# Sixteen-head attention: 1/sum applied to the head outputs on GpSimd instead of to the probabilities

## The chip, the cores and the metric

The kernel runs on one core of a Trainium2 chip. The metric is the device time of one execution, in microseconds (us); three runs of the kernel before gave 1747.81 us (median; 1742.91 to 1748.35). The change is judged by the median of the kernel after against that.

## What is computed

Four conditioned blocks follow one another on x of 16 batches x 256 rows x 256 columns, in float32. The change touches only the second one's attention, with 16 heads of 64:

```
h = _modulate(_layernorm(x), sh_msa, sc_msa)
q, k, v = jnp.split(h @ W_qkv, 3, axis=-1)               # to (batch, 256, 16 heads, 64)
attn = jax.nn.softmax(einsum('bqhd,bkhd->bhqk', q, k) * 64 ** -0.5, axis=-1)
out = einsum('bhqk,bkhd->bqhd', attn, v).reshape(batch, 256, 1024)
x = x + g_msa * (out @ W_out + b_out)
```

The softmax divides each row of exp(score - max) by the row's sum. A row belongs to one query q and one head, so the division may as well be made on that query's and head's output.

## The kernel before, in words

Five engines run instruction lists of their own and meet at semaphores: TensorE (PE), VectorE (DVE), ScalarE (ACT), GpSimd (POOL) and SyncE (SP, which issues all DMAs). Each list is in order: an instruction that waits holds up everything behind it on its engine. float32 matmuls are made of three passes over a high and a low part (`hi`, `lo`), so most results are read out of PSUM twice, by ACT (the `hi` copy) and by DVE (`lo` = value - `hi`).

The attention is written as a software pipeline of 128 periods, n = 8 b + j, for batch b and head pair j = 0 to 7. In period n each engine does, in this order:

- PE (`mh_tensor`): the first half of the transposes of pair n's probabilities (`pair_transpose`, L1086), the scores of pair n+2 (`pair_scores`, L1019), the other half of the transposes, the projections due in this period (q and k of one pair in each; in j = 1, 2, 5, 6 also a quarter of V), in j = 3 the transposes of the next batch's rows, the output projection of pair n-3, and the values of pair n-1 (`head_values`).
- ACT (`mh_scalar`, L1279): `o_read` of pair n-2 (L1148, two copies of 64 partitions out of PSUM into `oc`), `pt_read` of pair n (L1115, two), the four exponentials of pair n+2 (L1055; each also yields a row sum in `rsum`; in j = 3 `rows_scalar`, L1221, stands in the middle of them), then `proj_scalar`, the `hi` copies of the period's projections (L995 for q and k, L1003 for V).
- DVE (`mh_vector`, L1304): 1/sum of pair n+1 (`prob_inverse`, L1064), in j = 3 `res_vector` (L1186), the row maxima of pair n+2 (`score_max`, L1045), `o_add` of pair n-2 (two additions, L1157, then the rounded copy `oThi`, L1161), `pt_rest` of pair n (L1120, two), in j = 3 `rows_vector` (L1232, L1235), `proj_vector` (L1012, L1017), in j = 1 `ln_stats` (L353, L359), in j = 2 `ln_norm` (L376), in j = 4 `weights_hi` (L327).
- POOL (`mh_gpsimd`, L1339): four multiplications of the probabilities of pair n+1 by `rinv` (`prob_weigh`, L1083), and `o_rest` of pair n-2 (L1166), beside small work in j = 2 to 5. In the last two periods ACT does two of the four multiplications (`prob_weigh_act`, L1076).
- SP (`mh_sync`, L1363): only in j = 0, two weight slices (L313) and one gate row (L1209).

Waits that matter: the first transposes of a period wait for the weighed probabilities and for `pt_rest` of the pair before (`pt_lo`); the scores of pair n+2 wait for the exponentials of pair n+1 (their two PSUM banks are single); `score_max` waits for the scores; the exponentials wait for `score_max`; `o_add` waits for both copies of `o_read` (`o_corr`) and, one pair back, for `o_rest` (`o_lo`); `head_values` waits for the `o_add` of the pair before in the shared bank (`o_sum`).

Of the kernel before, what the change touches and what calls it, by code (L numbers as in the profile page):

```python
# [15 lines left out]
ALU = mybir.AluOpType  # L16
# [27 lines left out]
def bass_cond_blocks(nc, t, out):  # L44
# [57 lines left out]
    GROUP_BASE = before(lambda q: GROUPS if q in HID else 0)  # L102

    gate_scratch = nc.dram_tensor("gate_scratch", (NPH, BATCH, 2 * D), F32).ap()

    ctx = ExitStack()
    with ctx:
# [59 lines left out]
        rsum = [sb(f"rsum{i}", [P, 2 * TPB], scope=att) for i in range(2)]  # L167
        rinv = [sb(f"rinv{i}", [P, 2 * TPB], scope=att) for i in range(2)]


        front_a, front_b = DC * HID[0] + HID[0] // P * D, DC * HID[1] + HID[1] // P * D
# [51 lines left out]
        ln_xn = sem("ln_xn"); ln_tp = sem("ln_tp"); ln_nf = sem("ln_nf"); ln_lo = sem("ln_lo"); ln_full = sem("ln_full"); prob_act = sem("prob_act"); pt_half = sem("pt_half")  # L223
# [4 lines left out]
        x_new = sem("x_new"); x_tmp = sem("x_tmp"); x_stored = sem("x_stored")  # L228

        o_corr = sem("o_corr"); o_sum = sem("o_sum"); q_scaled = sem("q_scaled")  # L230
        proj_mm = sem("proj_mm"); proj_hi = sem("proj_hi"); proj_lo = sem("proj_lo")
        v_hi = sem("v_hi"); v_lo = sem("v_lo"); s_mm = sem("s_mm"); max_ready = sem("max_ready")
# [802 lines left out]

        def of_head(tiles, h):

            return tiles[h // 2 % 2][:, h % 2 * TPB:(h % 2 + 1) * TPB]

        def score_max(dve, n):  # L1040

# [6 lines left out]
        def score_exp(act, h):  # L1048

            act.wait_ge(nmax_ready, h - h % 2 + 2)  # L1050
            if h >= 4:
                act.wait_ge(pt_mm, h - 3)
                act.wait_ge(rinv_ready, h - h % 2 - 2)
# [12 lines left out]
        SHARED = 2  # L1066

        def weighed(h):

            return h - max(h // 2 - (PERIODS - SHARED), 0)  # L1070

        def prob_weigh_act(act, h):

            act.wait_ge(rinv_ready, h - h % 2 + 2)
            for q in range(TPB):
                last = act.activation(prob[h % 4][:, q, :], prob[h % 4][:, q, :], ACT.Copy, scale=of_head(rinv, h)[:, q:q + 1])  # L1076
            last.then_inc(prob_act, 1)

        def prob_weigh(pool, h):

            pool.wait_ge(rinv_ready, h - h % 2 + 2)
            for q in range(TPB):
                last = pool.tensor_scalar(prob[h % 4][:, q, :], prob[h % 4][:, q, :], of_head(rinv, h)[:, q:q + 1], None, ALU.mult)  # L1083
            last.then_inc(prob_ready, 1)

        def pair_transpose(pe, n, turn):  # L1086

            if n == 0:
                pe.wait_ge(y_taken, GB * GROUP_BASE[A])
            if turn == 0:  # L1090
                pe.wait_ge(prob_ready, weighed(2 * n + 2))
                if n >= PERIODS - SHARED:
                    pe.wait_ge(prob_act, n - (PERIODS - SHARED) + 1)
                if n:
                    pe.wait_ge(pt_lo, 2 * n)
            else:
                pe.wait_ge(pt_half, 2 * n + 2)
            for c in range(TPB):
                for q in range(TPB):
                    both = []  # L1100
                    for h in range(2):
                        r = (h + turn) % 2
                        rows = slice(r * HALF, (r + 1) * HALF)
                        at = c * SEQ + q * P + r * HALF
                        both.append(pe.transpose(PTB[h][:, at:at + HALF],  # L1105
                                                 prob[(2 * n + h) % 4][rows, q, c * P:(c + 1) * P], ident[rows, rows]))
            for ins in both:
                ins.then_inc(pt_mm if turn else pt_half, 1)
# [38 lines left out]
                main, rest, cols = o_halves(j)  # L1147
                act.activation(oc[main, :], OB[rest, cols], ACT.Copy).then_inc(o_corr, 1)  # L1148

        def o_add(dve, pair, i):  # L1150

            if pair:
                dve.wait_ge(o_lo, pair)
            for j in range(2):
                main, _, cols = o_halves(j)
                dve.wait_ge(o_corr, 2 * pair + 2)
                dve.tensor_tensor(of[main, :], OB[main, cols], oc[main, :], ALU.add).then_inc(o_sum, 1)  # L1157
            dve.wait_ge(o_sum, 2 * pair + 2)
            if pair >= 2:
                dve.wait_ge(out_mm, pair - 1)  # L1160
            dve.tensor_copy(oT[i][0][:, :], of[:, :]).then_inc(o_hi, 1)  # L1161

        def o_rest(pool, pair, i):

            pool.wait_ge(o_hi, pair + 1)
            pool.tensor_tensor(oT[i][1][:, :], of[:, :], oT[i][0][:, :].bitcast(F32),  # L1166
                               ALU.subtract).then_inc(o_lo, 1)

        def out_project(pe, pair, j, b):
# [109 lines left out]
        def mh_scalar(act, b, j):  # L1279

            n = PAIRS * b + j
            if n >= 2:
                o_read(act, n - 2)
            if PERIODS > n + 1 >= PERIODS - SHARED:
                prob_weigh_act(act, 2 * n + 3)
            for h in range(2):
                pt_read(act, 2 * n + h)
            if n + 2 < PERIODS:
                score_exp(act, 2 * n + 4)
            if j == NEXT - 1 and b + 1 < BATCH:  # L1290
                act.wait_ge(proj_mm, item(b, ("qk", PAIRS - 1)) + 1)
                rows_scalar(act, b + 1)
            if n + 2 < PERIODS:
                score_exp(act, 2 * n + 5)
            for it in items(b, j):
                proj_scalar(act, *it)
            if b == BATCH - 1 and j in (PAIRS - 3, PAIRS - 2):
                act.wait_ge(proj_mm, NPROJ * BATCH)
                head_unit("scalar", act, A + 1, j - (PAIRS - 3))
            if n == PERIODS - 1:  # L1300
                o_read(act, n - 1)
                o_read(act, n)

        def mh_vector(dve, b, j):  # L1304

            n = PAIRS * b + j
            if n + 1 < PERIODS:
                prob_inverse(dve, n + 1)
            if j == 3 and b:
                res_vector(dve, A, b - 1, YB, out_mm, PAIRS * b, b - 1)  # L1310
            if n + 2 < PERIODS:
                score_max(dve, n + 2)
            if n >= 2:
                o_add(dve, n - 2, n % 2)
            for h in range(2):
                pt_rest(dve, 2 * n + h)
            if j == NEXT - 1 and b + 1 < BATCH:
# [14 lines left out]
                for k in range(GB):  # L1332
                    head_unit("vector", dve, A + 1, k)
            if n == PERIODS - 1:
                o_add(dve, n - 1, (n - 1) % 2)
                o_add(dve, n, n % 2)
                res_vector(dve, A, b, YB, out_mm, PAIRS * b + PAIRS, b)

        def mh_gpsimd(pool, b, j):  # L1339

            n = PAIRS * b + j
            if n + 1 < PERIODS:
                prob_weigh(pool, 2 * n + 2)
            if j == 2 and b + 1 < BATCH:
                ln_rsqrt(pool, A, b + 1, 0)
            if b == BATCH - 1 and j == NEXT - 1:
                head_norms("gpsimd", pool, A + 1)
            if n + 1 < PERIODS - SHARED:
# [7 lines left out]
            if j == NEXT + 1:  # L1356
                res_gpsimd(pool, b, b)
            if n == PERIODS - 1:
                o_rest(pool, n - 1, (n - 1) % 2)
                o_rest(pool, n, n % 2)  # L1360
                res_add(pool, b, b)

        def mh_sync(sp, b, j):  # L1363

            if j:
                return
            weights_load(sp, A + 1, b)
            gate_load(sp, A, b, b)


        def mh_start(name, eng):
            if name == "gpsimd":
                for h in range(2):
                    prob_weigh(eng, h)
                return
            f = {"tensor": proj_tensor, "scalar": proj_scalar, "vector": proj_vector}[name]

# [13 lines left out]
            f(eng, 0, ("qk", 2))  # L1391
            if name == "tensor":
                pair_scores(eng, 1)
            if name == "vector":
                prob_inverse(eng, 0)
            head_pair(1)
            f(eng, 0, ("v", 0, 1))
            f(eng, 0, ("qk", 3))
# [28 lines left out]
        def sh_transpose(pe, b):  # L1427

            n = H0 + b
            pe.wait_ge(prob_ready, weighed(H0) + b + 1)  # L1430
# [32 lines left out]
        def sh_scale(dve, b):  # L1463

            dve.wait_ge(exp_ready, H0 + b + 1)
            dve.wait_ge(prob_ready, weighed(H0) + b - 1)
            if b >= 2:
                dve.wait_ge(prob_ready1, b - 1)
            dve.reciprocal(rinv[0][:, 0:TPB], rsum[0][:, 0:TPB]).then_inc(rinv_ready, 1)
            dve.wait_ge(rinv_ready, H0 + b + 1)  # L1470
# [332 lines left out]
```

## Time and profile before

| | us |
|---|---|
| median of three runs | 1747.81 |
| span of the profiled execution | 1752.5 |
| sixteen-head attention in it, about | 256 to 1012 |
| PE busy in the span | 1626.4 (93%) |
| DVE / ACT / POOL busy | 1294.3 / 1179.8 / 1093.6 |

The profile is of one execution. Besides totals it offers a chain of work that ended last (each step followed back to what released it), groups of instructions by line, a timeline by engine, and busy times of chosen stretches. The view of the DMAs gives issues and the time from issue to landing.

### The profile page before, as it was taken

What the parts mean: (1) busy time and instruction counts of PE and PEld (TensorE: products, weight loads), DVE (VectorE), ACT (ScalarE), POOL (GpSimd) and SP (SyncE); (2) the same over time, 40 slices, a digit from 0 to 9 for tenths busy, and PEclk for the clock granted to TensorE, in tenths of its full rate; (3) what the DMA queues carried; (4) which work ended last, traced back from release to release, by engine and by line L of the source; (5) the groups of instructions that cost most, each with busy time, mean ns of one, the idle gap of its engine ahead of it and who ended that gap; (6) DMA issues with size and microseconds to landing.
All of it is one profiled execution on the core that took longest, in us unless ns stands there. A gap on an engine that the chain in (4) does not pass through costs nothing.

```text
span 1752.5 us, 37390 instructions
## 1 busy us (share of the span) xinstructions
PE 1626.4 (93%) x13251; PEld 1458.4 (83%) x13251; DVE 1294.3 (74%) x2766; ACT 1179.8 (67%) x2896; POOL 1093.6 (62%) x1261
## 2 busy tenths in 40 slices
PE   4888998999999999999999789999999999989997
PEld 2557878888888888888888779999888889989997
DVE  3767768989898888888888745556788778864442
ACT  2545657777787777787777655556676667666663
POOL 1555667888888888888888622333555568842223
PEclk7999999999999999999999899999999999999999
DMA  8213310000000000000000011111122112221111
GB/s 306 61 49 86 88 42 11 11 10 11 11 7 6 11 10 11 11 11 11 10 11 10 1 32 30 31 31 32 48 57 58 45 27 46 47 52 37 37 49 48
DMA packets 110973, 65.93 MB, mean 38 GB/s; under 512 B 81530, under 2 KB 92788, under 8 KB 110788
## 3 DMA queue, kind: packets, MB, share of 16 engines
q1 hardware_dynamic: 110788, 63.54, 13.3%
q8 instruction: 107, 1.75, 0.4%
q14 instruction: 78, 0.64, 0.1%
HBM read 59.06 MB, written 4.46 MB: 36 GB/s over the span
## 4 chain that ended last, share of the span: by engine, by line
PE 64%; DVE 13%; issue 8%; POOL 6%; ACT 2%; DMA 0%; DVEq 0%; POOLq 0%; SPq 0%; ACTq 0%
PE bank L289 14%; PE bank L290 13%; PE bank L291 13%; POOL prob L1083 5%; PE s_banks L289 4%; PE bank L1105 4%; DVE ptlo L1120 4%; PE s_banks L290 4%; PE s_banks L291 4%; PE s_banks L1028 4%; PE bank L1131 3%; DVE of L1157 2%; PE bank L417 2%; DVE xn L376 2%; DVE oThi L1161 1%
## 5 line engine op out<-in xcount | busy, mean ns | idle before, releaser
L1083 POOL TENSOR_SCALAR prob<-prob,rinv 128x256 f32<-128x256 f32 x508 | 465.8, 935 | 117.0 <-DVE rinv L1064 117.0
L1055 ACT ACTIVATE prob<-s_banks,nmax 128x256 f32<-128x256 f32 x512 | 236.6, 475 | 17.4 <-DVE nmax L1045 17.4
L289 PE MATMUL bank<-WBhi,hl 128*128 128x256 f32 x768 | 219.0, 285 | 6.2 <-DVE upd L647 5.3
L290 PE MATMUL bank<-WBlo,hh 128*128 128x256 f32 x768 | 217.7, 283 | 0.0
L291 PE MATMUL bank<-WBhi,hh 128*128 128x256 f32 x768 | 215.5, 281 | 0.0
L1115 ACT ACTIVATE pthi<-bank 128x512 fp32r<-128x512 f32 x256 | 139.2, 596 | 100.9 <-PE bank L1105 98.8
L1045 DVE TENSOR_REDUCE nmax<-s_banks 128x4 f32<-128x1024 f32 x128 | 156.0, 1219 | 62.6 <-issue 61.9
L610 ACT ACTIVATE hh<-bank,vecs 128x512 fp32r<-128x512 f32 x120 | 82.9, 691 | 155.7 <-PE bank L291 155.7
L430 ACT ACTIVATE nThi<-bank,mod 128x256 fp32r<-128x256 f32 x192 | 110.5, 575 | 104.9 <-issue 75.7
L289 PE MATMUL bank<-aThi,WAlo 128*128 128x256 f32 x576 | 175.4, 304 | 0.6 <-DVE aTlo L438 0.2
L1120 DVE TENSOR_TENSOR ptlo<-bank,pthi 128x512 fp32r<-128x512 f32 x256 | 164.9, 686 | 4.0
L616 DVE TENSOR_TENSOR hl<-bank,hh 128x512 fp32r<-128x512 f32 x120 | 82.5, 688 | 112.3 <-ACT bank L610 111.2
L290 PE MATMUL bank<-aTlo,WAhi 128*128 128x256 f32 x576 | 161.6, 281 | 0.0
L289 PEld LDWEIGHTS bank<-WBhi,hl 128*128 128x128 f32 x768 | 145.8, 190 | 18.7 <-issue 9.7
L291 PE MATMUL bank<-aThi,WAhi 128*128 128x256 f32 x576 | 161.1, 280 | 0.0
L1105 PE MATMUL bank<-ident,prob 64*128 64x64 f32 x2048 | 113.9, 228 | 45.2 <-DVE ptlo L1120 23.4
L290 PEld LDWEIGHTS bank<-WBlo,hh 128*128 128x128 f32 x768 | 145.8, 190 | 7.2
L1105 PEld LDWEIGHTS bank<-ident,prob 64*128 64x128 f32 x2048 | 92.6, 139 | 67.1 <-POOL prob L1083 37.1
L376 DVE TENSOR_SCALAR xn<-x,meanvar,rstd 128x256 f32<-128x256 f32 x224 | 123.6, 610 | 31.4 <-POOL rstd L368 31.4
L291 PEld LDWEIGHTS bank<-WBhi,hh 128*128 128x128 f32 x768 | 146.5, 191 | 0.0
L1131 PE MATMUL bank<-ptlo,vv 128*128 128x256 f32 x512 | 129.8, 286 | 7.2 <-DVE of L1157 7.2
L616 DVE TENSOR_TENSOR hl<-s_banks,hh 128x512 fp32r<-128x512 f32 x120 | 81.6, 680 | 72.6 <-ACT s_banks L610 72.6
(185 smaller groups left out, 5546.5 us busy)
## 6 DMA issues: line engine op xcount, KB each, us to landing
gates<-gate_scratch SPq DMA_DIRECT2D x96, 256.0 KB, 3.6
agate<-gate_scratch SPq DMA_DIRECT2D x32, 256.0 KB, 3.6
stage<-in_L_cond_W SPq DMA_DIRECT2D x64, 64.0 KB, 2.3
out<-x SPq DMA_DIRECT2D x16, 256.0 KB, 2.2
adaw<-in_L_cond_Wc SPq DMA_DIRECT2D x1, 3072.0 KB, 17.7
stage<-in_L_cond_W_qkv SPq DMA_DIRECT2D x8, 384.0 KB, 3.4
x<-in_x SPq DMA_DIRECT2D x1, 2560.0 KB, 16.6
stage<-in_L_cond_ff_w SPq DMA_DIRECT2D x32, 64.0 KB, 2.2
```

The costliest lines, as they stand in the source:

```text
L289: pe.matmul(dst, lhs[1], rhs[0], start=start, stop=False, skip_group_check=True)
L290: pe.matmul(dst, lhs[0], rhs[1], start=False, stop=False, skip_group_check=True)
L291: return pe.matmul(dst, lhs[0], rhs[0], start=False, stop=stop, skip_group_check=True)
L376: last = eng.tensor_scalar(xn[j][:, k * D:(k + 1) * D], x[:, bass.ds(b * ROWW + k * D, D)], meanvar[:, j, k, 0:1], rstd[:, j, k:k + 1], AL ...
L616: dve.tensor_tensor(hl[r][:, :], U_BANKS[r][:, :], hh[r][:, :].bitcast(F32), ALU.subtract).then_inc(h_lo, 1)
L1045: dve.tensor_reduce(nmax[n % 2][:, :], s_banks[:, :, :].rearrange("p h (q k) -> p (h q) k", q=TPB), AX_X, ALU.max, negate=True).then_inc(n ...
L1055: last = act.activation(prob[h % 4][:, q, :], SB_[h % 2][:, q * SEQ:(q + 1) * SEQ], ACT.Exp, bias=of_head(nmax, h)[:, q:q + 1], accum_out= ...
L1083: last = pool.tensor_scalar(prob[h % 4][:, q, :], prob[h % 4][:, q, :], of_head(rinv, h)[:, q:q + 1], None, ALU.mult)
L1105: both.append(pe.transpose(PTB[h][:, at:at + HALF], prob[(2 * n + h) % 4][rows, q, c * P:(c + 1) * P], ident[rows, rows]))
L1115: act.activation(pt[h % 4][0][:, :], PTB[h % 2][:, :], ACT.Copy).then_inc(pt_hi, 1)
L1120: dve.tensor_tensor(pt[h % 4][1][:, :], PTB[h % 2][:, :], pt[h % 4][0][:, :].bitcast(F32), ALU.subtract).then_inc(pt_lo, 1)
L1131: last = pe.matmul(OB[:, h % 2 * SEQ:(h % 2 + 1) * SEQ], vv[:, c, h * P:(h + 1) * P], pt[h % 4][m][:, c * SEQ:(c + 1) * SEQ], start=c == 0 ...
```

## The change

The probabilities stay undivided. 1/sum of a pair (128 partitions x 4) is stored by SP into DRAM element by element, transposed, and loaded back as rows broadcast over the 64 partitions of each head. POOL multiplies the pair's head outputs by these rows, twice (once rounded to `oThi`, once in full to `on`), and then subtracts. The four multiplications of the probabilities and DVE's copy `oThi` go. Transposes wait for the exponentials instead of for the weighing. In DVE's list `prob_inverse` is of pair n instead of n+1, and `o_add` stands ahead of `score_max` instead of behind it. SP issues three DMAs in each period. `rsum` has four buffers instead of two, the rows and `on` lie in free words of `stage`. The other attention's waits (`sh_transpose`, `sh_scale`) are counted anew.

```diff
         def prob_inverse(dve, n):
             dve.wait_ge(exp_ready, 2 * n + 2)
             if n >= 2:
-                dve.wait_ge(prob_ready, 2 * n - 2)
-            dve.reciprocal(rinv[n % 2][:, :], rsum[n % 2][:, :]).then_inc(rinv_ready, 2)
+                dve.wait_ge(sums_stored, 16 * (n - 1))
+            dve.reciprocal(rinv[n % 2][:, :], rsum[n % 4][:, :]).then_inc(rinv_ready, 2)
+
+        def inverse_store(sp, n):
+            sp.wait_ge(rinv_ready, 2 * n + 2)
+            if n >= 2:
+                sp.wait_ge(rrow_loaded[n % 2], 32 * (n // 2))
+            sp.dma_start(sum_scratch[n % 2, :, :].rearrange("h (q p) -> p h q", p=P),
+                         rinv[n % 2][:, :].rearrange("p (h q) -> p h q", q=TPB),
+                         allow_slow_non_contiguous=True).then_inc(sums_stored, 16)
+
+        def inverse_load(sp, n):
+            sp.wait_ge(sums_stored, 16 * (n + 1))
+            if n >= 2:
+                sp.wait_ge(o_lo, n - 1)
+            for h in range(2):
+                sp.dma_start(rrow[n % 2][h * HALF:(h + 1) * HALF, :],
+                             sum_scratch[n % 2, h:h + 1, :].to_broadcast([HALF, SEQ])).then_inc(rrow_loaded[n % 2], 16)
...
             if turn == 0:
-                pe.wait_ge(prob_ready, weighed(2 * n + 2))
-                if n >= PERIODS - SHARED:
-                    pe.wait_ge(prob_act, n - (PERIODS - SHARED) + 1)
+                pe.wait_ge(exp_ready, 2 * n + 2)
                 if n:
                     pe.wait_ge(pt_lo, 2 * n)
...
-        def o_add(dve, pair, i):
+        def o_add(dve, pair):
...
                 dve.wait_ge(o_corr, 2 * pair + 2)
                 dve.tensor_tensor(of[main, :], OB[main, cols], oc[main, :], ALU.add).then_inc(o_sum, 1)
-            dve.wait_ge(o_sum, 2 * pair + 2)
+
+        def o_scale(pool, pair, i):
+            pool.wait_ge(o_sum, 2 * pair + 2)
+            pool.wait_ge(rrow_loaded[pair % 2], 32 * (pair // 2 + 1))
             if pair >= 2:
-                dve.wait_ge(out_mm, pair - 1)
-            dve.tensor_copy(oT[i][0][:, :], of[:, :]).then_inc(o_hi, 1)
+                pool.wait_ge(out_mm, pair - 1)
+            pool.tensor_tensor(oT[i][0][:, :], of[:, :], rrow[pair % 2][:, :], ALU.mult).then_inc(o_hi, 1)
+            if pair:
+                pool.wait_ge(o_lo, pair)
+            pool.tensor_tensor(on[:, :], of[:, :], rrow[pair % 2][:, :], ALU.mult).then_inc(o_scaled, 1)
...
         def mh_vector(dve, b, j):
             n = PAIRS * b + j
-            if n + 1 < PERIODS:
-                prob_inverse(dve, n + 1)
+            prob_inverse(dve, n)
             if j == 3 and b:
                 res_vector(dve, A, b - 1, YB, out_mm, PAIRS * b, b - 1)
+            if n >= 2:
+                o_add(dve, n - 2)
             if n + 2 < PERIODS:
                 score_max(dve, n + 2)
-            if n >= 2:
-                o_add(dve, n - 2, n % 2)
             for h in range(2):
                 pt_rest(dve, 2 * n + h)
...
         def mh_gpsimd(pool, b, j):
-            if n + 1 < PERIODS:
-                prob_weigh(pool, 2 * n + 2)
...
-            if n + 1 < PERIODS - SHARED:
-                prob_weigh(pool, 2 * n + 3)
             if n >= 2:
+                o_scale(pool, n - 2, n % 2)
                 o_rest(pool, n - 2, n % 2)
...
         def mh_sync(sp, b, j):
-            if j:
-                return
-            weights_load(sp, A + 1, b)
-            gate_load(sp, A, b, b)
+            n = PAIRS * b + j
+            if j == 0:
+                weights_load(sp, A + 1, b)
+                gate_load(sp, A, b, b)
+            inverse_store(sp, n)
+            inverse_load(sp, n)
```

## Rows read from the trace of the kernel before

**Rows 1.** Page, the chain that ended last: share of the span by engine.

```profile
PE 64%; DVE 13%; issue 8%; POOL 6%; ACT 2%; DMA 0%; DVEq 0%; POOLq 0%; SPq 0%; ACTq 0%
```

**Rows 2.** Stretches: the steady attention, period j = 6, then j = 7 (from:to, length, busy).

```profile
270.00:967.00 697.00, 657.87 (x6882) 609.82 (x6881) 623.42 (x1198) 551.57 (x1647) 586.68 (x689) 1.00 0.05 10
...
481.67:487.73 6.06, 6.06 (x65) 5.58 (x60) 4.99 (x9) 4.73 (x14) 5.20 (x7) 1.00 0.01 3
487.73:492.98 5.25, 4.71 (x58) 4.49 (x54) 4.40 (x9) 4.25 (x13) 4.12 (x6) 1.00 0.00 0
```

**Rows 3.** Timeline of DVE: the row maxima of one batch (start, duration; idle before).

```profile
457.74 1.22 DVE L1045 TENSOR_REDUCE nmax<-s_banks 128x4 f32<-128x1024 f32 x1
...
464.26 1.21 DVE L1045 TENSOR_REDUCE nmax<-s_banks 128x4 f32<-128x1024 f32 x1
...
470.29 1.19 DVE L1045 TENSOR_REDUCE nmax<-s_banks 128x4 f32<-128x1024 f32 x1
...
475.62 1.23 DVE L1045 TENSOR_REDUCE nmax<-s_banks 128x4 f32<-128x1024 f32 x1 [0.41 <-issue]
...
481.67 1.23 DVE L1045 TENSOR_REDUCE nmax<-s_banks 128x4 f32<-128x1024 f32 x1 [0.96 <-issue]
...
487.73 1.23 DVE L1045 TENSOR_REDUCE nmax<-s_banks 128x4 f32<-128x1024 f32 x1 [0.97 <-issue]
...
492.98 1.22 DVE L1045 TENSOR_REDUCE nmax<-s_banks 128x4 f32<-128x1024 f32 x1 [0.75 <-issue]
...
498.10 1.22 DVE L1045 TENSOR_REDUCE nmax<-s_banks 128x4 f32<-128x1024 f32 x1 [0.64 <-issue]
...
504.18 1.23 DVE L1045 TENSOR_REDUCE nmax<-s_banks 128x4 f32<-128x1024 f32 x1
```

**Rows 4.** Timeline of DVE in period j = 7, behind the maximum at 487.73.

```profile
488.88 0.86 DVE L1157 TENSOR_TENSOR of<-bank,oc 64x256 f32<-64x256 f32 x2
489.77 0.41 DVE L1161 CAST oThi<-of 128x256 fp32r<-128x256 f32 x1
...
491.45 0.69 DVE L1012 TENSOR_TENSOR qklo<-bank,qkhi 128x512 fp32r<-128x512 f32 x1
```

**Rows 5.** Timeline of PE: first transposes of the period that follows.

```profile
491.65 0.46 PE L1105 MATMUL bank<-ident,prob 64*128 64x64 f32 x8 [0.54 <-DVE ptlo L1120]
```

**Rows 6.** Timeline of ACT in j = 7: the q and k copy, then `o_read`.

```profile
490.81 0.61 ACT L995 ACTIVATE qkhi<-bank 128x512 fp32r<-128x512 f32 x1
491.44 0.78 ACT L1148 ACTIVATE oc<-bank 64x256 f32<-64x256 f32 x2
```

**Rows 7.** Groups of POOL's instructions, 270 to 967 us (count | busy, mean ns).

```profile
L1083 POOL TENSOR_SCALAR prob<-prob,rinv 128x256 f32<-128x256 f32 x480 | 440.3, 935 | 105.1 <-DVE rinv L1064 105.1
...
L1166 POOL TENSOR_TENSOR oTlo<-of,oThi 128x256 fp32r<-128x256 f32 x120 | 88.2, 735 | 0.0
```

**Rows 8.** Timelines: DVE and ACT ahead of the next maximum, j = 1, 3, 4, 6.

```profile
503.97 0.14 DVE L1064 RECIPROCAL rinv<-rsum 128x4 f32<-128x4 f32 x1
...
466.42 1.02 ACT L1221 ACTIVATE aThi<-bank,mod 128x256 fp32r<-128x256 f32 x2
...
467.97 1.00 DVE L1232 TENSOR_SCALAR bank<-bank,mod 128x256 f32<-128x256 f32 x2
...
475.05 0.16 DVE L1064 RECIPROCAL rinv<-rsum 128x4 f32<-128x4 f32 x1
...
486.60 0.17 DVE L1064 RECIPROCAL rinv<-rsum 128x4 f32<-128x4 f32 x1
```

**Rows 9.** One line, 262 to 1000 us: durations (ns min/median/max).

```profile
L376 DVE TENSOR_SCALAR xn<-x,meanvar,rstd x34: 401/548/757, 276.9 to 985.5; 128x256 f32<-128x256 f32 x34
```

**Rows 10.** SP's issues of two weight slices; line L313's time to landing, 260 to 960 us.

```profile
382.83 0.88 SPq L313 DMA_DIRECT2D stage<-in_L_cond_W  x2
...
DMA to landing us min/median/max: 1.9/2.3/3.5
```

**Rows 11.** The chain that ended last, at the start of the attention (start, length).

```profile
256.13 3.64 POOL prob L1083 x4
```

More of the change, by code:

```diff
@@ L104, in bass_cond_blocks @@
     gate_scratch = nc.dram_tensor("gate_scratch", (NPH, BATCH, 2 * D), F32).ap()
+    sum_scratch = nc.dram_tensor("sum_scratch", (2, 2, SEQ), F32).ap()
     ctx = ExitStack()
@@ L166, in bass_cond_blocks @@
         nmax = [sb(f"nmax{i}", [P, 2 * TPB], scope=att) for i in range(2)]
-        rsum = [sb(f"rsum{i}", [P, 2 * TPB], scope=att) for i in range(2)]
+        rsum = [sb(f"rsum{i}", [P, 2 * TPB], scope=att) for i in range(4)]
         rinv = [sb(f"rinv{i}", [P, 2 * TPB], scope=att) for i in range(2)]
+        SLICE_WORDS = 256
+        rrow = [stage[:, SLICE_WORDS + i * SEQ:SLICE_WORDS + (i + 1) * SEQ] for i in range(2)]
+        on = stage[:, SLICE_WORDS + 2 * SEQ:SLICE_WORDS + 3 * SEQ]
         front_a, front_b = DC * HID[0] + HID[0] // P * D, DC * HID[1] + HID[1] // P * D
@@ L228, in bass_cond_blocks @@
         x_new = sem("x_new"); x_tmp = sem("x_tmp"); x_stored = sem("x_stored")
+        sums_stored = sem("sums_stored"); rrow_loaded = [sem(f"rrow_loaded{i}") for i in range(2)]; o_scaled = sem("o_scaled")
         o_corr = sem("o_corr"); o_sum = sem("o_sum"); q_scaled = sem("q_scaled")
@@ L1052, in score_exp @@
                 act.wait_ge(pt_mm, h - 3)
-                act.wait_ge(rinv_ready, h - h % 2 - 2)
+            if h >= 8:
+                act.wait_ge(rinv_ready, h - h % 2 - 6)
             for q in range(TPB):
@@ L1062, in prob_inverse @@
             if n >= 2:
-                dve.wait_ge(prob_ready, 2 * n - 2)
-            dve.reciprocal(rinv[n % 2][:, :], rsum[n % 2][:, :]).then_inc(rinv_ready, 2)
[L1066 to L1084, printed above, removed]
+                dve.wait_ge(sums_stored, 16 * (n - 1))
[14 more added lines that the diff above has]
+                             sum_scratch[n % 2, h:h + 1, :].to_broadcast([HALF, SEQ])).then_inc(rrow_loaded[n % 2], 16)
         def pair_transpose(pe, n, turn):
@@ L1334, in mh_vector @@
             if n == PERIODS - 1:
-                o_add(dve, n - 1, (n - 1) % 2)
-                o_add(dve, n, n % 2)
+                o_add(dve, n - 1)
+                o_add(dve, n)
                 res_vector(dve, A, b, YB, out_mm, PAIRS * b + PAIRS, b)
@@ L1358, in mh_gpsimd @@
             if n == PERIODS - 1:
-                o_rest(pool, n - 1, (n - 1) % 2)
-                o_rest(pool, n, n % 2)
+                for m in (n - 1, n):
+                    o_scale(pool, m, m % 2)
+                    o_rest(pool, m, m % 2)
                 res_add(pool, b, b)
         def mh_sync(sp, b, j):
-            if j:
-                return
-            weights_load(sp, A + 1, b)
-            gate_load(sp, A, b, b)
+            n = PAIRS * b + j
[4 more added lines that the diff above has]
+            inverse_load(sp, n)
         def mh_start(name, eng):
             if name == "gpsimd":
-                for h in range(2):
-                    prob_weigh(eng, h)
                 return
@@ L1393, in mh_start @@
                 pair_scores(eng, 1)
-            if name == "vector":
-                prob_inverse(eng, 0)
             head_pair(1)
@@ L1429, in sh_transpose @@
             n = H0 + b
-            pe.wait_ge(prob_ready, weighed(H0) + b + 1)
+            pe.wait_ge(prob_ready, b + 1)
             pe.wait_ge(prob_ready1, b + 1)
@@ L1465, in sh_scale @@
             dve.wait_ge(exp_ready, H0 + b + 1)
-            dve.wait_ge(prob_ready, weighed(H0) + b - 1)
+            if b == 0:
+                dve.wait_ge(sums_stored, 16 * PERIODS)
             if b >= 2:
+                dve.wait_ge(prob_ready, b - 1)
                 dve.wait_ge(prob_ready1, b - 1)
```

9 lines of the change are left out of this document (4 added, 5 removed).

## Prediction, before the change was built

> **What bounds the kernel now.** I read the chain that ended last first: 64% of the span is PE, but DVE has 13% and POOL 6% [rows 1]. In the steady attention PE is busy 657.87 of 697 us at a granted clock of 1.00 [rows 2], so perfect cover of everything else could free 39 us of it, less what is modelled. The stretches by period show where: a period with a quarter of V (j = 6) is 6.06 us long with PE busy for all of it, one without (j = 7) is 5.25 with PE busy 4.71 [rows 2].
>
> The pace is best read on one instruction that stands once in each period: DVE's maximum [rows 3]. From start to start the eight distances of a batch are, from j = 2 on, 6.52, 6.03, 5.33, 6.05, 6.06, 5.25, 5.12 and 6.08, together 46.44 us. What ends each is seen in the idle notes: in front of five of the nine maxima DVE waits 0.41 to 0.97 us (for the scores), in front of the others it comes straight from other work. So j = 1, 2, 3 are at DVE's pace, j = 5, 6 at PE's, and j = 4, 7, 0 at a circle: in j = 7 the maximum at 487.73 is followed by `o_add` at 488.88, `oThi` at 489.77 and the two `ptlo` [rows 4]; only then may the next transposes go, which come 0.54 us after PE was free [rows 5], then scores, then the next maximum.
>
> **What goes.** POOL's four multiplications of 0.935 a period [rows 7] and PE's waits for them, DVE's `oThi` (0.41, from 489.77 [rows 4]). POOL then has three operations of L1166's size, 3 x 0.735 = 2.2 us a period where it had 4 x 0.935 + 0.735 = 4.5 [rows 7]. The transposes of pair n wait for exponentials made two periods earlier, which costs nothing. This alone would leave PE as the bound (first rival).
>
> **What is moved.** `o_add` now stands ahead of the maximum. It needs both copies of `o_read`, and ACT makes these only after the exponentials and `hi` copies of the period before: in j = 7 the q and k copy starts at 490.81, and `o_read` follows at 491.44 without idle [rows 6]. The exponentials in turn wait for the maximum. This closes a circle over two engines: maximum, exponentials, `hi` copies (ACT), `o_read` (ACT), `o_add` (DVE), next maximum. Before, the maximum was ahead of `o_add`, and `o_add`, `oThi` and `ptlo` ran beside the exponentials; the q and k `lo` came 491.45 - 487.73 = 3.72 after the maximum with no gap [rows 3, 4]. Now `ptlo` follows the maximum at once and DVE sits idle until ACT hands over the q and k copy, and ACT later waits for DVE. I work out each distance anew, from rows of the old run:
> - j = 7 and 0: `o_read` ends at 491.44 + 0.78 = 492.22, that is 4.49 after the maximum [rows 3, 6]. ACT to DVE takes 0.03 (copy ends 491.42, `qklo` starts 491.45 [rows 4, 6]); `o_add` keeps DVE 489.77 - 488.88 = 0.89 [rows 4]. 4.49 + 0.03 + 0.89 = 5.41 (5.25 and 5.12 before).
> - j = 1: `ln_stats` fills DVE, rinv at 503.97 and the maximum at 504.18 come without idle [rows 3, 8]; `o_add` goes in front: 6.08 + 0.89 = 6.97.
> - j = 2: the same with `ln_norm`: 6.52 + 0.89. Its two L376 took 0.548 each in the middle and 0.401 at best [rows 9]; with POOL mostly idle I take 0.2 off: 7.2.
> - j = 3: `ptlo` no longer delays `rows_vector`, which can start when ACT's copies end, 466.42 + 1.02 = 467.44, 3.18 after the maximum; from L1232's start to the maximum was 470.29 - 467.97 = 2.32 of unbroken work [rows 3, 8]. 3.18 + 0.03 + 2.32 + 0.89 = 6.42 (6.03 before).
> - j = 4: rinv at 475.05 was 4.76 after the maximum [rows 3, 8]; about 0.1 for it and 0.89 give 5.75 (5.33 before).
> - j = 5, 6: rinv at 486.60 was 4.93 after the maximum [rows 3, 8]; plus 0.1 and 0.89, 5.92. PE's own need is 6.06 [rows 2], partly caught up in the longer periods before: 6.0.
>
> Sum: 2 x 5.41 + 6.97 + 7.2 + 6.42 + 5.75 + 2 x 6.0 = 49.16, against 46.44: +2.7 us a batch, 15 batches +41.
>
> A rule of the Trainium skill bears on the 0.2. "SBUF — State Buffer", section "SBUF: two separate sides", says that a DVE instruction in a two-port mode and a GpSimd instruction lock one shared port pair in turn. L376's spread [rows 9] fits; by the rule its whole excess over the shortest run would go, 0.29 instead of 0.2, and the batch would come to 49.07.
>
> **Edges.** The first transposes waited 3.64 us for POOL [rows 11]; the first two periods have no or little `o_add`; in the last batch most projections are missing, and ACT's two weighings go. Against that the last pair's outputs pass two multiplications more and one copy less, 2 x 0.735 - 0.41 = +1.1 [rows 4, 7]. Bounds: two such POOL waits saved at either end, some -7, and +2. Most of the saved waits is not lost time, since exponentials and scores hold the same periods: I take -4.
>
> **What is added and should cost nothing.** SP: a store and two loads a period. An issue takes 0.88 / 2 = 0.44, a landing 1.9 to 3.5 [rows 10]; these slices go in up to 1024 pieces of 64 bytes, the store in 512 of 4 bytes, a size that no row shows. Store to loads is a wait in SP's own list: 0.44 + 3.5 + 0.88 + 0.2 for handovers = 5.0 at the longest landing seen, under the 6.1 of a mean period. The rows are needed two periods later: the loads wait for `o_rest` of pair n-2 (2.5 us behind its `o_add`), then 0.88 + 3.5; 6.9 of the 12.3 us that lie between the two `o_add`. The weight and gate loads of j = 0 stand ahead of one store (1.3 us, inside this slack). New waits: `prob_inverse` for a store two periods old, with `o_add` and the maximum queued behind it; `o_add` for `o_rest` one period old (2.5 of 5.4 us); the output projections likewise. `rsum` with four buffers leaves the exponentials free. If the cover on SP goes, the case is the third rival. PE's values wait for `o_add`, now earlier. I leave the clock at 1.00.
>
> **Sum.** +41 - 4 = +37. The profiled execution has 1752.5, so 1789.5; it stands 4.7 (0.27%) above the median of the runs, so 1747.8 + 37 = 1785.
>
> **The rivals.** (a) Faster: PE becomes the bound. If `o_add` fits in the wait for the scores, no maximum is later, and the periods without V fall to PE's 4.71 (j = 3 to some 5.2 with its transposes): 3 x 4.71 + 5.2 + 4 x 6.06 = 43.6, -2.9 a batch, about 1703. For it: the 0.64 to 0.97 of idle in front of five maxima [rows 3] is nearly an `o_add`. Against: it needs `o_read` done about 0.9 before the scores, and ACT has it only behind the `hi` copies, with no gap [rows 6]. It decides where ACT runs ahead by a microsecond; I see no such place but the edges. Chance 0.08.
> (b) Level: the three short periods gain what j = 1 to 3 lose, 1743 to 1753. Chance 0.04.
> (c) The store is slow and SP sets the pace: store, landing L, two issues and handovers are L + 1.5 a period. It decides from L = 4.6; at L = 6 each of some 126 periods has 7.5 instead of 6.1, +170, about 1955. For it: 4-byte pieces; against: 1024 pieces land within 3.5 [rows 10]. Chance 0.06.
> For (c) speaks the Trainium skill, "DMA: Bandwidth & Descriptors", sections "Rules for kernel authors" (a strided last dim becomes one descriptor for each element) and "Specifications" (under 512 bytes a read-modify-write); no run here shows a 4-byte store yet.
>
> **How the numbers follow.** My forecast has 0.82: slower, 1785. Its unknowns: handovers of 0.03 to 0.2 in five places, j = 5, 6 between 5.92 and 6.06, L376 with 0 to 0.3: 48.8 to 50.0 a batch, +35 to +54; the edges -7 to +2; and 0.1 us that I may misjudge in each of eight distances, 12 us in all. +16 to +64: 1764 to 1812. That holds nearly all of the forecast; (a), (b) and (c), 0.18, are left out. About 0.3% (5 us) is what a measurement here can tell from no change: faster 0.09 (a and a little of b), same 0.05, slower 0.86.
>
> **What would show it.** Right: POOL out of the chain, ACT's `oc` and DVE's `of` in it; DVE idle between `ptlo` and `qklo` about 1.2 us a period, and maxima with `of` directly ahead; distances of 5.4 in j = 7 and 0, about 7 in j = 1 and 2; PE's waits at the first transposes gone, its idle time at the scores. Wrong: maxima that wait for scores, PE busy through j = 7 (a); POOL's first multiplication waiting for DMA (c).

## The result, and the profile after

The changed kernel takes 2464.57 us (median of 4 runs, 2457.32 to 2469.43) where the kernel before took 1748.08 (median of 4): 1.408 times as long, 95% interval 1.4049 to 1.4111. The forecast was 1785, at most 1812. The sign was right; the cause and the size were not. The profiled execution took 2467.74, its span is 2465.9.

The chain that ended last, by engine and by line, from the page of the changed kernel:

```profile
DMA 52%; PE 30%; SPq 7%; issue 3%; DVE 3%; ACT 1%; POOL 1%; POOLq 0%; DVEq 0%; ACTq 0%
DMA sum_scratch<-rinv 51%; PE bank L294 7%; PE bank L295 7%; PE bank L296 7%; SPq L1087 5%; PE s_banks L294 3%; PE s_banks L295 3%; PE s_banks L296 3%; PE bank L422 2%; DVE xn L381 1%; SPq L318 1%; SPq L1219 0%; PE bank L482 0%; ACT bank L615 0%; PE bank L1440 0%
```

DMA had 0% of that chain before [rows 1]. It now has 52%, and nearly all of it is one transfer, the store of `rinv` into `sum_scratch`. SP's timeline (start, duration) shows how it gets there:

```profile
1002.46 0.54 SPq L1077 DMA_DIRECT2D sum_scratch<-rinv  x1
1013.67 1.08 SPq L1087 DMA_DIRECT2D stage<-sum_scratch  x2
1014.85 0.54 SPq L1077 DMA_DIRECT2D sum_scratch<-rinv  x1
1024.06 2.05 SPq L1087 DMA_DIRECT2D stage<-sum_scratch  x2
1026.20 0.54 SPq L1077 DMA_DIRECT2D sum_scratch<-rinv  x1
```

The chain in the same stretch (start, length), which counts from the store's issue:

```profile
1002.46 11.20 DMA sum_scratch<-rinv
...
1014.85 9.19 DMA sum_scratch<-rinv
...
1026.20 8.76 DMA sum_scratch<-rinv
```

SP's waits over the whole run (total, times, longest):

```profile
SPq L1087 <- DMA sum_scratch<-rinv: 1204.3, 128, 11.1
```

SP issues a store (L1077), waits until it has landed, issues the two loads that need it (L1087), and goes straight to the next store. It waits 1204.3 / 128 = 9.41 us for each of the 128 stores. With 0.54 for the store's issue, 1.1 to 2.0 for the loads' and 0.1 to 0.2 of handover a round is some 11.5 us: from the first store, at 260.0, to the 128th, at 1714.6, it is 11.45 on average. SP has no time to spare in it. A pair of heads took 46.44 / 8 = 5.8 us before [rows 3].

Everything else queues up behind SP. The waits from 600 to 1600 us (engine, tile and line, released by; total, times, longest):

```profile
POOL oThi L1167 <- issue: 749.5, 88, 16.7
ACT prob L1061 <- DVE nmax L1050: 542.8, 87, 8.8
DVE rinv L1070 <- DMA sum_scratch<-rinv: 453.9, 88, 7.1
```

POOL waits at its first multiplication, in 88 pairs 749.5 us. "issue" says that this view found no releaser; the trace's landing records name it: in 127 of the 128 pairs POOL starts 0.12 to 0.17 us after the last landing of its rows. DVE's reciprocal waits for a store two pairs old to free the buffer, and `o_add` and the maximum stand in line behind it, so ACT's exponentials wait for the maximum. The stretches of this window and of that in [rows 2] (from:to, length, busy of PE, PEld, DVE, ACT, POOL; granted clock, DMA share, GB/s):

```profile
600.00:1600.00 1000.00, 691.58 (x5018) 622.67 (x5017) 435.25 (x786) 401.77 (x1196) 235.40 (x330) 0.77 0.17 17
270.00:967.00 697.00, 483.66 (x3554) 436.06 (x3553) 307.25 (x558) 284.14 (x844) 163.60 (x230) 0.77 0.17 17
```

In the same 697 us PE executes 3554 matmuls, where before it executed 6882 [rows 2]: the attention runs at half its rate. No engine is the bound, and neither is the DMA engines' throughput, busy for 17%. The bound is one transfer of 2 KB whose landing is long, standing in a serial list. Most of that time is not spent on moving the pieces: of the store issued at 1002.46 the profile has the last packet before 1004.5, from 1004.5 to 1013.6 it has no DMA packet at all, and the store lands at 1013.66. The granted clock fell from 1.00 to 0.77, a mean over stretches at full speed (2.4 GHz, 1.00) and at half (1.2 GHz, 0.50); PE is busy for 69% of this stretch, where it was for 94%. DMA and SP make up the chain here, so the lower clock costs nothing more.

### The profile page after: what moved, and what is told of

Read it like the earlier page. It is cut to its first block, busy times and chain, and to the rows that moved or that the text cites. A ratio compares the mean times of both kernels' runs of the same rounds, so it can differ in the third digit from the quotient of the medians.

```text
span 2465.9 us, 37771 instructions
## 1 busy us (share of the span) xinstructions
PE 1923.2 (78%) x13251; PEld 1706.4 (69%) x13251; DVE 1265.6 (51%) x2638; ACT 1179.5 (48%) x2892; POOL 811.4 (33%) x1009
## 4 chain that ended last, share of the span: by engine, by line
DMA 52%; PE 30%; SPq 7%; issue 3%; DVE 3%; ACT 1%; POOL 1%; POOLq 0%; DVEq 0%; ACTq 0%
DMA sum_scratch<-rinv 51%; PE bank L294 7%; PE bank L295 7%; PE bank L296 7%; SPq L1087 5%; PE s_banks L294 3%; PE s_banks L295 3%; PE s_banks L296 3%; PE bank L422 2%; DVE xn L381 1%; SPq L318 1%; SPq L1219 0%; PE bank L482 0%; ACT bank L615 0%; PE bank L1440 0%
## 5 line engine op out<-in xcount | busy, mean ns | idle before, releaser
L1167 POOL TENSOR_TENSOR oThi<-of,stage 128x256 fp32r<-128x256 f32 x128 | 93.3, 729 | 1074.2 <-issue 1063.9
L1133 PE MATMUL bank<-ptlo,vv 128*128 128x256 f32 x512 | 168.6, 350 | 187.8 <-DVE of L1159 187.7
L1133 PEld LDWEIGHTS bank<-ptlo,vv 128*128 128x128 f32 x512 | 122.1, 238 | 204.6 <-issue 204.3
L1107 PE MATMUL bank<-ident,prob 64*128 64x64 f32 x2048 | 153.4, 285 | 124.1 <-DVE ptlo L1122 123.8
L294 PE MATMUL bank<-aThi,WAlo 128*128 128x256 f32 x576 | 223.4, 388 | 0.1
L295 PE MATMUL bank<-aTlo,WAhi 128*128 128x256 f32 x576 | 202.4, 351 | 0.0
L294 PE MATMUL bank<-WAhi,oTlo 128*128 128x256 f32 x256 | 84.8, 331 | 134.7 <-POOL oTlo L1176 95.0
L294 PEld LDWEIGHTS bank<-aThi,WAlo 128*128 128x128 f32 x576 | 151.2, 263 | 13.9 <-issue 0.2
L1133 PE MATMUL bank<-pthi,vv 128*128 128x256 f32 x512 | 160.5, 334 | 0.0
L294 PEld LDWEIGHTS bank<-WAhi,oTlo 128*128 128x128 f32 x256 | 55.7, 218 | 149.7 <-POOL oTlo L1176 118.0
```

What stands on the lines that cost most here:

```text
L294: pe.matmul(dst, lhs[1], rhs[0], start=start, stop=False, skip_group_check=True)
L295: pe.matmul(dst, lhs[0], rhs[1], start=False, stop=False, skip_group_check=True)
L1107: both.append(pe.transpose(PTB[h][:, at:at + HALF], prob[(2 * n + h) % 4][rows, q, c * P:(c + 1) * P], ident[rows, rows]))
L1133: last = pe.matmul(OB[:, h % 2 * SEQ:(h % 2 + 1) * SEQ], vv[:, c, h * P:(h + 1) * P], pt[h % 4][m][:, c * SEQ:(c + 1) * SEQ], start=c == 0 ...
L1167: pool.tensor_tensor(oT[i][0][:, :], of[:, :], rrow[pair % 2][:, :], ALU.mult).then_inc(o_hi, 1)
```

## The experiments

**1. Is it the transfers alone?** The changed kernel, with stores and loads for the first two pairs only; its later pairs are multiplied by rows of other pairs.

```
  def inverse_store(sp, n):
+     if n >= 2:
+         return
  def inverse_load(sp, n):
+     if n >= 2:
+         return
  (waits of rinv and of o_scale: the counts of the first two pairs)
```

> The changed kernel, but the store and the loads of 1/sum are made for the first two pairs only; later pairs are multiplied by those rows (values that do not belong to them), and nothing waits for a transfer. Everything else is as in the changed kernel. Theory 'the store sets the pace, and behind it stands the circle of maximum, exponentials, o_read and o_add': the 9.4 us waits of SP vanish and the time falls from 2465 to what the prediction worked out without a DMA wait, about 1785 (1764 to 1812), with maxima 5.4 us apart in j = 7 and 0 and about 7 in j = 1 and 2. Rival 'without the store TensorE is the bound': about 1703 to 1715, PE busy through j = 7. Rival 'the store was not it': stays near 2465.

Measured: 1791.64 against 1750.54, ratio 1.0228 (1.0205 to 1.025). So 673 of the 716 us (2464.57 - 1748.08) come with the transfers, and without them the kernel lands in the forecast's range. DVE's timeline in j = 7 and 0 (start, duration; idle before):

```profile
503.01 1.23 DVE L1050 TENSOR_REDUCE nmax<-s_banks 128x4 f32<-128x1024 f32 x1
504.27 1.29 DVE L1126 TENSOR_TENSOR ptlo<-bank,pthi 128x512 fp32r<-128x512 f32 x2
506.73 0.69 DVE L1017 TENSOR_TENSOR qklo<-bank,qkhi 128x512 fp32r<-128x512 f32 x1 [1.17 <-ACT qkhi L1000]
507.34 0.17 DVE L1070 RECIPROCAL rinv<-rsum 128x4 f32<-128x4 f32 x1
507.61 0.88 DVE L1163 TENSOR_TENSOR of<-bank,oc 64x256 f32<-64x256 f32 x2
508.51 1.23 DVE L1050 TENSOR_REDUCE nmax<-s_banks 128x4 f32<-128x1024 f32 x1
...
514.01 1.23 DVE L1050 TENSOR_REDUCE nmax<-s_banks 128x4 f32<-128x1024 f32 x1
```

This is the predicted circle: `ptlo` at once behind the maximum, 1.17 us idle until ACT's q and k copy, `o_add` directly ahead of the next maximum. ACT's timeline closes it, the exponentials waiting for the maximum:

```profile
506.09 0.61 ACT L1000 ACTIVATE qkhi<-bank 128x512 fp32r<-128x512 f32 x1
506.72 0.78 ACT L1154 ACTIVATE oc<-bank 64x256 f32<-64x256 f32 x2
509.77 0.47 ACT L1061 ACTIVATE prob<-s_banks,nmax 128x256 f32<-128x256 f32 x1 [1.04 <-DVE nmax L1050]
```

`oc` ends at 507.50 and `of` starts at 507.61. The eight distances, j = 2 to 7, 0, 1, are 7.13, 6.44, 5.63, 6.07, 6.06, 5.50, 5.50 and 6.82, together 49.15 us.

**2. The order alone, in the kernel before.** Only `o_add`'s additions go ahead of the maximum; the rounded copy stays behind it. No transfer and no multiplication is moved.

```
+     if n >= 2:
+         o_add(dve, n - 2, n % 2)
      if n + 2 < PERIODS:
          score_max(dve, n + 2)
      if n >= 2:
-         o_add(dve, n - 2, n % 2)
+         o_round(dve, n - 2, n % 2)
```

> The kernel before with one part of the change alone: the two additions of o_add stand ahead of score_max in VectorE's list; the rounded copy oThi stays behind score_max. No DMA is added, GpSimd still weighs the probabilities. Theory 'the order alone closes a circle over VectorE and ScalarE': 49.2 to 49.5 us a batch instead of 46.4, about +43 us, 1790 (1770 to 1805). Rival 'the additions fit into the wait for the scores': 1743 to 1753.

Measured: 1787.12 against 1750.54, ratio 1.0208 (1.0182 to 1.0234). The distances of a batch sum to 49.10. Two lines of one function are worth 36.6 us. The waits from 270 to 967 us:

```profile
ACT prob L1055 <- DVE nmax L1045: 126.4, 114, 1.8
DVE qklo L1012 <- ACT qkhi L995: 92.9, 100, 1.3
```

The two halves of the circle are now DVE's and ACT's largest waits. Before, in the same window:

```profile
ACT prob L1055 <- DVE nmax L1045: 14.8, 31, 0.7
DVE qklo L1012 <- ACT qkhi L995: 1.3, 1, 1.3
```

**3. The order, without the transfers.** Experiment 1 with `score_max` ahead of `o_add` again.

> As the run without transfers after the first two pairs (later pairs are multiplied by those rows, values that are not theirs), but with score_max ahead of o_add as in the kernel before. Theory 'the order is the whole of the 40 us': periods become the old ones without oThi, without the weighing's waits: 44.4 us a batch (j = 7, 0, 4: 4.8 to 4.9; j = 1, 2, 5, 6: 6.06; j = 3: 5.7), about 1713 (1700 to 1725). Rival 'GpSimd's longer way to the output halves costs as well': near 1748 or above.

Measured: 1719.08 against 1748.39, ratio 0.9825 (0.9803 to 0.9847). With the maximum first the rest of the change gains 29 us; with the change's order it is +41, with that order alone (experiment 2) +37. So under this order nothing is left of the gain, and here the order costs 1791.6 - 1719.1 = 72.5 us. The steady attention, as in [rows 2]:

```profile
270.00:967.00 697.00, 682.13 (x7113) 635.35 (x7113) 597.60 (x1123) 570.11 (x1704) 336.25 (x466) 0.99 0.05 11
```

PE is busy for 682 of 697 us and does 7113 matmuls where it did 6882 [rows 2]. A batch takes 44.4 us. This is rival (a)'s bound, PE, reached by another order than the change has.

**4. What makes the store slow: its pieces.** The store writes 512 words of 4 bytes, one for each partition and column, to 2 KB of DRAM without gaps. Two kernels change the target. The first writes the 4 columns of a partition as one piece, 128 pieces of 16 bytes, still without gaps; the loads then read the words in a wrong order:

```
- sp.dma_start(sum_scratch[n % 2, :, :].rearrange("h (q p) -> p h q", p=P),
-              rinv[n % 2][:, :].rearrange("p (h q) -> p h q", q=TPB), ...)
+ sp.dma_start(sum_scratch[n % 2, :, :].rearrange("h (p f) -> (h p) f", f=2 * TPB),
+              rinv[n % 2][:, :])
```

> The changed kernel with the store written as 128 pieces of 16 bytes in the order of the partitions instead of 512 pieces of 4 bytes; the loads then take the words in a wrong order, nothing else differs. Theory 'the pieces cost' (by number, or by engines that meet in the same stretch of DRAM): landing 2 to 3 us, SP's round 4.5 to 5.5 us, no longer the bound, about 1785. Rival 'a fixed wait, or the loads queued ahead of the store': landing stays 9 us, about 2465.

The second keeps 512 pieces of 4 bytes and puts them 512 bytes apart; its loads read another tensor:

```
- sum_scratch = nc.dram_tensor("sum_scratch", (2, 2, SEQ), F32).ap()
+ sum_scratch = nc.dram_tensor("sum_scratch", (2, 2, SEQ, 128), F32).ap()
```

> The changed kernel, its store still 512 pieces of 4 bytes, but each to a stretch of 512 bytes of its own in a larger scratch; the loads read rows of another tensor in DRAM of the same size, so the multiplied values are not the sums. Theory 'each piece costs, wherever it goes': landing stays about 9 us, 2465 (2400 to 2520). Rival 'pieces that share a stretch of DRAM hold each other up': landing 2 to 4 us, about 1785.

Measured: 1788.0 (ratio 1.021 to 1750.54), and 1793.28 against 1750.54 in a single run: both as without transfers. The stores' time to landing, of the 128 x 16 bytes and then of the spread pieces:

```profile
DMA to landing us min/median/max: 1.4/2.1/6.1
```

```profile
DMA to landing us min/median/max: 1.7/2.0/4.1
```

So neither the 4-byte size nor the number 512 is slow by itself: 512 pieces of 4 bytes land in 2.0 us when they lie apart.

**5. Half of the packed pieces.** The changed kernel with one head's 256 words stored; both loads read these.

> The changed kernel, the store halved: one head's 256 pieces of 4 bytes into one row of 1024 bytes (both heads are then multiplied by that head's row). As many pieces as before fall into each stretch of 512 bytes, half as many in all. Theory 'pieces that fall into the same stretch go one after the other, different stretches side by side': landing stays near 9 us, about 2400. Rival 'all pieces of a store go one after the other once they share stretches': landing near 5.5 us, SP's round 7.5 us, about 1960.

Measured: 2346.32 against 1748.39 (a single run); SP waits 1079.8 / 128 = 8.44 us for each, where it waited 9.41. Half of the pieces save a tenth of the wait. The view that the store's time goes with its number of pieces falls.

**6. Is it the reading back?** In experiment 4 the spread store's loads read another tensor. The control is the changed kernel's store, packed (its pieces without gaps), with the same loads, and then pieces 32 and 8 bytes apart (the tensor's last dimension 1, 8 and 2 words).

> A control for the run with the spread store: the store as in the changed kernel (512 pieces of 4 bytes, packed), the loads from the other tensor in DRAM, so the multiplied values are not the sums. Theory 'the packed store alone takes long': landing 9 us, about 2465. Rival 'reading back what was just written takes long': landing 2 to 3 us, about 1790.

> As the control, the pieces 32 bytes apart, so that 16 of them share a stretch of 512 bytes instead of 128 (packed) or one (spread run); the multiplied values are not the sums. Theory 'pieces of one stretch go one after the other, some 60 ns each': 16 take 1 us, landing about 3 us, SP's round 5 us, about 1790. Rival 'any sharing of 512 bytes costs the whole wait': about 2465.

> The changed kernel with the 512 four-byte pieces of each store 8 bytes apart in DRAM, and with loads that read a stretch of another tensor (its rows are foreign values). Packed, a store landed in 9.07 us (i_spread1); 32 bytes apart, in 2.2. If only pieces that touch each other hold each other up, 8 bytes apart is as quick as 32: landing about 2.2 and 1790 us in all. If the pieces share a stretch of 32 bytes and take their turns in it (8 packed, 4 here), about half of the excess stays: landing 5 to 6, SP's round about 7.5, some 1950 us. If any neighbours within 32 bytes hold each other up in full, 9 us and 2430 again.

Measured, in single runs: 2428.21 packed, 1790.01 at 32 bytes (both against 1751.0), 1793.69 at 8 bytes (against 1755.19). Packed, SP waits:

```profile
SPq L1087 <- DMA sum_scratch<-rinv: 1160.7, 128, 10.8
```

That is 9.07 us each with nothing read back, so the store alone is slow. Its stores from 480 to 520 us are issued at 483.87, 493.86, 504.91 and 515.55, each right behind two loads. The DMA engines' busy share in this stretch, one digit for each microsecond, in tenths:

```profile
DMA  0000140000000006000000000441000000000460
```

Each burst is over 2.1 to 3.3 us after the store's issue, and six or more empty microseconds follow until SP's next transfer. At 32 and at 8 bytes the landings were:

```profile
DMA to landing us min/median/max: 1.8/2.2/6.0
```

```profile
DMA to landing us min/median/max: 3.1/4.4/7.6
```

At 8 bytes the landing lies between the two ends, as the middle expectation had it in kind (5 to 6 expected, 4.4 measured); the 1950 us that went with it did not come, because SP's round still fits. Its timeline in this run has stores at:

```profile
479.78 0.54 SPq L1077 DMA_DIRECT2D sum_scratch<-rinv  x1
483.73 1.38 SPq L1087 DMA_DIRECT2D stage<-gate_scratch  x2
485.20 1.45 SPq L1077 DMA_DIRECT2D sum_scratch<-rinv  x1
489.47 1.09 SPq L1087 DMA_DIRECT2D stage<-gate_scratch  x2
491.92 0.36 SPq L1077 DMA_DIRECT2D sum_scratch<-rinv  x1
```

Rounds of 5.42 and 6.72 us follow the pairs' pace of 6.1. The point from which rival (c) decides, L = 4.6, holds from below: at a median landing of 4.4 it costs next to nothing.

**7. Hiding the store by a longer lag.** Complete versions with the packed store as it is: `rinv` one period earlier and with four buffers, the loads of pair n - 1 issued behind the store of pair n + 1, so that SP waits for a store that has had a whole round to land (the first and the last period's lines are left out here). Once with the maximum first, once with the change's order.

```
-     inverse_store(sp, n)
-     inverse_load(sp, n)
+     if n + 1 < PERIODS:
+         inverse_store(sp, n + 1)
+     if n:
+         inverse_load(sp, n - 1)
```

> A version that computes all of it: 1/sum one period earlier, rinv and the scratch with four buffers and a semaphore each, the loads of pair n-1 issued behind the store of pair n+1, so that SP no longer stands still for each landing and two stores are under way; score_max ahead of o_add. Theory 'a store takes 9 us to land but two can overlap': 1705 to 1730, faster than both kernels. Rival 'stores into DRAM go one after the other, 9 us each': about 2300 to 2465.

> The same lagged transfers with the order of the changed kernel (o_add ahead of score_max). Theory 'the store was all of the loss beyond the order': about 1790, as without transfers. Rival 'stores one after the other': 2300 to 2465.

Measured: 1851.57 (ratio 1.0581, 1.0547 to 1.0615) and 1892.65 (1.0817), both against 1748.39. The stores overlap, and at the change's order 2464.57 - 1892.65 = 572 us are gone; but both are over 100 us above what I expected. In the first, the waits from 270 to 967 us:

```profile
POOL oThi L1167 <- issue: 188.8, 40, 9.4
...
DVE nmax L1050 <- issue: 79.3, 62, 4.7
```

SP's own waits for the loads over the whole run:

```profile
SPq L1076 <- DMA stage<-sum_scratch: 116.9, 63, 7.7
```

and SP's timeline:

```profile
717.47 0.36 SPq L1077 DMA_DIRECT2D sum_scratch<-rinv  x1
717.93 3.97 SPq L1087 DMA_DIRECT2D stage<-sum_scratch  x2
722.12 0.41 SPq L1077 DMA_DIRECT2D sum_scratch<-rinv  x1
722.67 1.91 SPq L1087 DMA_DIRECT2D stage<-sum_scratch  x2
```

The issue of two transfers, 0.88 us before the change [rows 10] and 1.1 to 2.0 in the changed kernel, takes up to 3.97 right behind a store in this stretch, and POOL still waits up to 9.4 us. What I had overlooked is that the loads share the way with the next store, which is as slow as the last. The changed kernel's trace shows such a case: of the 32 landing records of the two loads issued from 1024.06 on, 31 come by 1028.11, and the last at 1034.50, among those of the next store (1030.25 to 1034.96). From 1028.0 to 1034.6 the profile has no DMA packet, so a queue of packets in the DMA engines is not what is seen. Where the loads wait stays open, and no run separates the next store from other causes.

**8. Both faults mended.** A complete version: the store as 128 pieces of 16 bytes in partition order, the loads (not printed here) bring the words of both heads to each half, POOL's multiplication picks its words with a step of four, and the maximum is ahead of `o_add`. SP's order is that of the change.

```
- sp.dma_start(sum_scratch[n % 2, :, :].rearrange("h (q p) -> p h q", p=P), ...)
+ sp.dma_start(sum_scratch[n % 2, :].rearrange("(p f) -> p f", f=2 * TPB), rinv[n % 2][:, :])
...
+ inv = rrow[pair % 2][:, :].rearrange("d (p h q) -> d h q p", h=2, q=TPB)[:, 0, :, :]
+ pool.tensor_tensor(dst, of, inv, ALU.mult)          (dst and of in the same order)
...
-     if n >= 2:
-         o_add(dve, n - 2)
      if n + 2 < PERIODS:
          score_max(dve, n + 2)
+     if n >= 2:
+         o_add(dve, n - 2)
```

> A version that computes all of it: the store is 128 pieces of 16 bytes in the order of the partitions (2.1 us to land in the run that had it), the loads bring all 512 words to each half (the second half from two words further on), and GpSimd's multiplications read them with a stride of four words; score_max ahead of o_add. SP keeps the plain order store, wait, loads. Theory 'with a quick store and the old order only the gain of the change is left': as without transfers, 1719, or a little above, 1715 to 1730, some 1.5% faster than the kernel before. Rival 'strided reads on GpSimd or the larger loads (2 KB a partition) become the wait': 1740 or more.

Measured: 1718.31 against 1751.0, ratio 0.9816 (0.98 to 0.9832): 1.8% less than the kernel before, with an interval clear of no change, and level with experiment 3, which has no transfers. The chain by engine on its page:

```profile
PE 79%; DVE 6%; ACT 3%; issue 3%; POOL 1%; DMA 1%; SPq 0%; POOLq 0%; DVEq 0%; ACTq 0%
```

The steady attention, as in [rows 2]:

```profile
270.00:967.00 697.00, 681.10 (x7092) 633.93 (x7091) 599.61 (x1120) 571.26 (x1708) 372.03 (x467) 0.99 0.25 57
```

SP's wait for the store over the whole run:

```profile
SPq L1090 <- DMA sum_scratch<-rinv: 64.5, 38, 5.0
```

And POOL's groups of multiplications, 270 to 967 us (count | busy, mean ns | idle before):

```profile
L1167 POOL TENSOR_TENSOR oThi<-of,stage 128x256 fp32r<-128x256 f32 x63 | 55.0, 873 | 116.5 <-DVE of L1162 116.5
...
L1167 POOL TENSOR_TENSOR stage<-of,stage 128x256 f32<-128x256 f32 x62 | 54.6, 880 | 0.0
```

SP waits for a store only 38 times, 64.5 us in all; the store's median landing is 2.8 us here. The step of four makes POOL's multiplication 873 to 881 ns instead of 729, which its idle time covers. PE has 79% of the chain, where it had 64% [rows 1].

## Why the prediction was wrong

**The step that failed** is "what is added and should cost nothing", in the store's landing L. I bounded it by 3.5 us, the longest landing of weight slices [rows 10], which go in pieces of 64 bytes, 1024 of them against 512 here. Those rows are of loads into SBUF. A store that writes neighbouring words of DRAM from many partitions had no row, and I let the nearest one stand as the upper end, which it had no reason to be. From a store's issue to the loads it is 8.0 to 11.8 us, on average 0.54 + 9.41 = 9.95. SP's round became 11.45 instead of 5.0, against a pace of 6.15, and 126 x (11.45 - 6.15) = 668 us; experiment 1 gives back 2464.6 - 1791.6 = 673.

**Rival (c)** had the mechanism, its place (SP's own list) and its threshold, L + 1.5 a pair, deciding from 4.6; with L = 9.95 its formula gives 11.45, the measured round. What failed in it is the assumed L = 6, a number that no row bounded, and the chance of 0.06. A size that no row shows, in a list where one instruction waits for another's landing, deserved more than that, and a range whose upper end lay where such a store would put it.

The two sections of the Trainium skill, "DMA: Bandwidth & Descriptors", that the prediction named for (c) point the right way, a strided last dimension and pieces under 512 bytes. The runs are narrower: 512 pieces of 4 bytes that lie apart land in 2.0 us, so descriptors of this size and number are not the cost here, and pieces 32 bytes apart, also under 512, are quick.

**What held.**
- The circle: 49.16 us a batch predicted, 49.15 in experiment 1, each distance within 0.15 of its own (j = 7 and 0: 5.41 predicted, 5.50; j = 1: 6.97 and 6.82; j = 3: 6.42 and 6.44; j = 4: 5.75 and 5.63). That the sums agree to 0.01 is luck: the misses have both signs. Experiment 2 shows that the order alone makes it.
- POOL's multiplication: 0.735 taken, 0.729 measured. Loads of rows: 3.5 taken, a median of 3.7 measured in the changed kernel, but 11.9 at most.
- The edges, in part: -4 taken, which made +37 in all. Experiment 1 has 1791.64 - 1750.54 = +41, and 15 batches of +2.71 are +41 alone, so the edges came to about 0, inside their bounds of -7 to +2.
- L376, L381 in the new numbering: I took 0.2 us off for a mostly idle POOL; in experiment 1 the line's durations (ns min/median/max) are

```profile
L381 DVE TENSOR_SCALAR xn<-x,meanvar,rstd x30: 404/406/410, 278.5 to 970.6; 128x256 f32<-128x256 f32 x30
```

against 401/548/757 before [rows 9]. The rule in the Trainium skill's "SBUF — State Buffer", section "SBUF: two separate sides", that the two engines lock one port pair in turn, fits the trace: the whole excess is gone, 0.28 us for two, as the rule had it and not 0.2 as I chose. How busy POOL is does not decide it, but whether the two meet. In experiment 2 POOL still weighs the probabilities, busy for 553 of 697 us, and L376 takes 403/407/411: its two run from 472.87 to 473.60, while POOL is idle from 472.62 to 473.79. Before, the first of two started at 462.66, while L1166 ran on POOL from 462.46 to 463.20, and took 0.69; the second took 0.40.

**Rival (a)** was wrong for this order: in experiment 1 every maximum comes directly behind `o_add`, and none waits for scores. Its bound is real, though. With the maximum first and cheap transfers a batch takes 44.4 us (it had 43.6), and the time is 1718 to 1719 (1703).

**Two slips** in the prediction change nothing here. The idle in front of the five maxima is 0.41 to 0.97, as its first use says, and not 0.64 to 0.97 as under (a). And the upper end of the range, by its own terms, is +54 + 2 + 12 = +68, that is 1816, and not +64; the result lies far above both.

## What to carry to other kernels

Before a transfer goes into a queue where the next instruction waits for its landing, ask whether any row shows a transfer of that direction, piece size and layout; if none does, the upper end of its price is open, and so is that of the forecast. Small results that go to DRAM and come back went quickly here when written as one piece for each partition in partition order, and sorted out where they are read (experiment 8); single words without gaps were the slow layout. An operation that is moved ahead of another on an in-order engine is to be followed through the other engines back to itself: here it closed a circle of 5.5 us that cost 36.6 us alone and 72.5 in the changed kernel without transfers.

## What the runs showed of the hardware

The landing of a small store went with how closely its 4-byte pieces lie, not with how many there are. SP's waits begin behind the issue (0.54 us); the other times count from the issue, medians where one number stands:

| store | pieces | from issue to landing (us) |
|---|---|---|
| 2 KB without gaps, 4 bytes each | 512 | 8.0 to 11.8 until the loads; SP's wait 9.41 |
| the same, loads from another tensor | 512 | SP's wait 9.07 |
| 1 KB without gaps, 4 bytes each | 256 | 9.1; SP's wait 8.44 |
| 4 bytes each, 8 bytes apart | 512 | 4.4 |
| 4 bytes each, 32 bytes apart | 512 | 2.2 |
| 4 bytes each, 512 bytes apart | 512 | 2.0 |
| 2 KB without gaps, 16 bytes each | 128 | 2.1 (2.8 in experiment 8, with larger loads) |

Twice the distance about halves the time, four times that again brings it to 2.2, near the least of these stores, 2.0, and half as many pieces at the same density save a tenth. A reading that fits all seven rows, though no run shows it at work, is that the pieces of one stretch of DRAM take turns, with the stretches side by side and some 2 us that any of these stores takes. By it such a stretch has at least 16 bytes, since two pieces 8 bytes apart still hold each other up, and at most 1 KB, since 1 KB alone is nearly as slow as 2 KB. The waiting is not in the DMA packets that the profile records: for the store issued at 1002.46 they end before 1004.5, and it lands at 1013.66. What in the chip makes the pieces wait stays open.
